# Layer-1 weight streams: the up weights of the feed-forward stage move from SP plus a VectorE cast to a casting load on POOL, the query weights of attention the other way

## What is computed

```
xn = layernorm(x)                                   # 2048 tokens x 1024
qkv = xn @ W_qkv + b_qkv                            # 16 heads of 64
s = softmax(q k^T / 8 + causal mask) v @ W_out + b_out
gate = xn @ (w_gate/127).T ; up = xn @ (w_up/127).T  # w_*: int32, hidden 3072
g = silu( (silu(gate) * up) @ (w_down/127).T )
x = x + s * g
```

## Time and profile before

| | |
|---|---|
| timed runs, median of 3 | 5059.19 us (5056.44, 5059.19, 5265.64) |
| the profiled execution | 4858.27 us, span of its slowest core 4856.6 us |
| spans of the eight cores | 4834.3 to 4856.6 us, mean granted clock 0.902 to 0.918 |
| TensorE busy | 3579.9 us, 74% |
| VectorE / ScalarE / POOL busy | 1320.2 / 1328.9 / 258.5 us |
| B1, gate and up steps of the first half | 3356 to 3560 us |
| C1, heads | 4147 to 4811 us |

### The profile page before, as it was taken

The page is one execution under the profiler, slowest core; times in us unless marked ns, Lnnn a source line. Parts: engine busy times, 40 slices in busy tenths (PEclk is TensorE's granted clock), DMA queues, the critical chain, the costliest instruction groups (busy, mean ns, idle before and its releaser), DMA issues.

```text
span 4856.6 us, 44207 instructions; the slowest of 8 cores (4834.3 to 4856.6 us)
## 1 busy us (share of the span) xinstructions
PE 3579.9 (74%) x14422; PEld 1437.2 (30%) x14712; DVE 1320.2 (27%) x2124; ACT 1328.9 (27%) x1573; POOL 258.5 (5%) x474
## 2 busy tenths in 40 slices
PE   2246666799999999986777777734798876667776
PEld 0012222344444444432222222211343332122222
DVE  3333320033023113203222222234212112454433
ACT  1100000011011011103666666511111100356663
POOL 1000000000000000000000000010000000000000
PEclk9868888899999999998999999856999999899998
DMA  2256778744434434440011121144343321122212
GB/s 74 65 147 192 199 208 188 188 147 146 140 131 147 139 139 140 146 124 11 11 31 37 35 42 37 37 112 107 87 96 72 87 53 28 18 52 53 49 36 65
DMA packets 139087, 463.50 MB, mean 95 GB/s; under 512 B 15568, under 2 KB 15728, under 8 KB 122480
## 3 DMA queue, kind: packets, MB, share of 16 engines
q0 software_dynamic: 66720, 205.83, 20.7%
q1 hardware_dynamic: 72144, 254.84, 15.5%
HBM read 490.23 MB, written 73.40 MB: 116 GB/s over the span
## 4 chain that ended last, share of the span: by engine, by line
PE 55%; DMA 15%; DVE 14%; ACT 9%; issue 5%; DVEq 1%; another core or an unknown queue 1%; SPq 0%; ACTq 0%; POOL 0%; POOLq 0%
PE pst L747 8%; ACT a16t L1539 8%; PE pst L761 8%; PE pst L863 4%; PE pb L863 4%; DMA a32t<-l_u 4%; PE pst L952 4%; PE pst L963 3%; PE pb L1016 3%; PE pb L1479 3%; PE pst L1505 2%; PE pst L1510 2%; DMA a16t<-s_g 2%; PE pb L1484 2%; PE pst L1393 2%
## 5 line engine op out<-in xcount | busy, mean ns | idle before, releaser
L1539 ACT ACTIVATE a16t<-pst 128x1024 bf16<-128x1024 f32 x832 | 852.1, 1024 | 452.5 <-PE pst L1510 379.1
L747 PE MATMUL pst<-xn_sb,a16t 128*128 128x512 bf16 x2256 | 585.4, 403 | 200.5 <-DVE a16t L695 165.3
L761 PE MATMUL pst<-xn_sb,a16t 128*128 128x512 bf16 x2259 | 552.6, 386 | 2.8 <-issue 0.7
L782 DVE TENSOR_TENSOR a32t<-a32t,pst 128x512 f32<-128x512 f32 x256 | 176.2, 688 | 1120.9 <-PE pst L761 1107.6
L774 ACT ACTIVATE a32t<-pst 128x512 f32<-128x512 f32 x288 | 172.0, 597 | 1106.0 <-PE pst L747 1090.6
L1479 PE MATMUL pb<-a16t 128*65 128x512 bf16 x832 | 332.9, 400 | 178.4 <-DVE a16t L1556 89.7
L1505 PE MATMUL pst<-a16t 128*128 128x512 bf16 x799 | 325.3, 407 | 159.9 <-DVE a16t L1438 103.4
L747 PEld LDWEIGHTS pst<-xn_sb,a16t 128*128 128x128 bf16 x2304 | 226.6, 102 | 509.8 <-issue 286.3
L1510 PE MATMUL pst<-a16t 128*128 128x512 bf16 x819 | 334.7, 409 | 6.6 <-DVE a16t L1452 4.1
L1484 PE MATMUL pb<-a16t 128*65 128x512 bf16 x832 | 330.9, 398 | 0.0
L761 PEld LDWEIGHTS pst<-xn_sb,a16t 128*128 128x128 bf16 x2304 | 229.9, 100 | 288.5 <-issue 29.5
(11 more groups left out here) (156 smaller groups left out, 2734.5 us busy)
## 6 DMA issues: line engine op xcount, KB each, us to landing
a16t<-s_g POOLq DMA_DIRECT2D x108, 512.0 KB, 4.9
a16t<-s_u SPq DMA_DIRECT2D x108, 512.0 KB, 3.7
a32t<-l_u SPq DMA_DIRECT2D x32, 1024.0 KB, 10.5
a16t<-s_d SPq DMA_DIRECT2D x27, 1024.0 KB, 5.4
a16t<-s_d POOLq DMA_DIRECT2D x27, 1024.0 KB, 5.8
a32t<-l_u SPq DMA_DIRECT2D x48, 512.0 KB, 4.9
s_g<-a16t SPq DMA_DIRECT2D x36, 512.0 KB, 7.9
s_u<-a16t SPq DMA_DIRECT2D x36, 512.0 KB, 8.5
```

Of the source, the lines that this page charges most:

```text
L747: li = t.matmul(pb[gp_][:, :], a16t[:, o_gb[wp] + hc * 256 + ici * 128: o_gb[wp] + hc * 256 + ici * 128 + 128], xn_sb[:, hc * T + tc * TC: ...
L761: li = t.matmul(pb[up_][:, :], a16t[:, o_ub[wp] + hc * 256 + ici * 128: o_ub[wp] + hc * 256 + ici * 128 + 128], xn_sb[:, hc * T + tc * TC: ...
L1539: return s.activation(a16t[:, o_pt[kp4]:o_pt[kp4] + 2 * TC], pst[kp][:, 0:1024], AF.Exp, scale=0.125)
```

## The change

In B1 the up tile is loaded by POOL straight to bf16, directly behind the gate tile and on the same semaphore, waiting like it for the h of step ic-2. The two staging buffers and the 48 casts are gone, and SP issues no load in B1.

In C1 the query weights are loaded by SP as f32 into the one scratch area `o_rt`. The load waits for the previous pair's cast (and at qi = 0 for the end of B1). A cast on VectorE then writes the bf16 tile; it waits for the load and for what the POOL load waited for. The operations are added where the POOL load was added: on SP behind the store of the previous pair's group, on VectorE behind the previous pair's fuse and ahead of L1447. The projection waits for the cast. Layer 0 keeps its load. `sWu` is an existing pair of semaphores.

```diff
-            o_st1 = [a32.alloc(1024) for _ in range(2)]
...
-                    def f_ldur(q, usrc=usrc, wp=wp):
+                    def f_ldu(q, usrc=usrc, wp=wp):
                         if q is None:
                             return 1
                         return q.dma_start(
-                            out=a32t[:, o_st1[wp]:o_st1[wp] + 1024].bitcast(I32),
-                            in_=usrc)
+                            out=a16t[:, o_ub[wp]:o_ub[wp] + 1024], in_=usrc)
...
-                    opldur = P.add("Q", f_ldur,
-                                   deps=[prev.get(("st1", wp))] + fen,
-                                   sem=sWu[wp], name=f"B1ldur{sc}.{ic}")
-
-                    def f_ucast(v, wp=wp):
-                        with nc.allow_low_precision(reason="i32 weight -> bf16"):
-                            return v.tensor_copy(
-                                a16t[:, o_ub[wp]:o_ub[wp] + 1024],
-                                a32t[:, o_st1[wp]:o_st1[wp] + 1024].bitcast(I32))
-                    opldu = P.add("V", f_ucast, deps=[opldur, bp],
-                                  name=f"B1ucast{sc}.{ic}")
-                    prev[("st1", wp)] = opldu
+                    opldu = P.add("G", f_ldu, deps=[bp] + fen, sem=sW[wp],
+                                  name=f"B1ldu{sc}.{ic}")
...
                     dlq = [pv.get(("qbuf", qi - 2))]
                     if qc == 0 and p < 2:
                         dlq.append(pv.get(("kbuf", nkv - 2 + p)))
-                    opldq = P.add("G", f_ldwq, deps=dlq, sem=sQW[p % 2],
-                                  name=f"C{L}ldq{qc}.{p}")
+                    if L == 0:
...
+                    else:
+                        def f_ldwqr(q, qsrc=qsrc):
+                            if q is None:
+                                return 1
+                            return q.dma_start(
+                                out=a32t[:, o_rt:o_rt + 1024], in_=qsrc)
+                        dqr = [pv.get(("qstg",))]
+                        if qi == 0:
+                            dqr = dqr + fence
+                        opldqr = P.add("Q", f_ldwqr, deps=dqr, sem=sWu[p % 2],
+                                       name=f"C1ldqr{qc}.{p}")
+
+                        def f_qwc(v, wp=wp):
+                            with nc.allow_low_precision(reason="wq f32 -> bf16"):
+                                return v.tensor_copy(
+                                    a16t[:, o_wq[wp]:o_wq[wp] + 1024],
+                                    a32t[:, o_rt:o_rt + 1024])
+                        opldq = P.add("V", f_qwc, deps=[opldqr] + dlq,
+                                      name=f"C1qwc{qc}.{p}")
+                        pv[("qstg",)] = opldq
```

More of the change, by code:

```diff
@@ L1378, in phase_C @@
                     qsrc = wq_src[p]
[L1380 to L1384, removed]
                     dlq = [pv.get(("qbuf", qi - 2))]
@@ L1387, in phase_C, with f_ldwq @@
                         dlq.append(pv.get(("kbuf", nkv - 2 + p)))
-                    opldq = P.add("G", f_ldwq, deps=dlq, sem=sQW[p % 2],
-                                  name=f"C{L}ldq{qc}.{p}")
+                    if L == 0:
+                        def f_ldwq(q, qsrc=qsrc, wp=wp):
+                            if q is None:
+                                return 1
+                            return q.dma_start(
+                                out=a16t[:, o_wq[wp]:o_wq[wp] + 1024], in_=qsrc)
+                        opldq = P.add("G", f_ldwq, deps=dlq, sem=sQW[p % 2],
+                                      name=f"C{L}ldq{qc}.{p}")
+                    else:
+                        def f_ldwqr(q, qsrc=qsrc):
+                            if q is None:
+                                return 1
+                            return q.dma_start(
+                                out=a32t[:, o_rt:o_rt + 1024], in_=qsrc)
[12 more added lines that the diff above has]
+                        pv[("qstg",)] = opldq
                     def f_qmm(t, wp=wp, qc=qc):
```

## The result

The changed kernel is slower: the ratio to the kernel before is 1.031 (95% interval 1.029 to 1.032). Each kernel was timed ten times: the medians are 5061.5 us (lowest 4999.6) and 4960.0 us (lowest 4846.3). Both medians contain executions in which one die of the chip ran at a lower clock, in shares that differ from kernel to kernel, so the ratio is taken from the undisturbed ones, which lie at 4846 to 4864 us before and at 5000 to 5012 us after: about 149 us more.

What follows compares the result with a forecast made beforehand. TensorE, busy 74% of the span, was taken as the bound, through its stops. B1 -80, C1 transfer +162, chunk 0 +5 and clock +46 gave +133 us, added to the 5059.2 us median: 5192 us, range 5120 to 5265.

Steps and rivals of the forecast that it cites:

- the last of the sum: Whole kernel: adds the same 133 us to the 5059.2 us median of three timed runs, giving 5192 us.
- B1, -80 us: Gate and up steps of B1: the wait for the cast goes, 1.74 us won in each of 46 steps.
- The term L: B1: time from POOL's first load issue to the landing of the second load, estimated at 5.7 us.
- the formula's two steps: B1: with two alternating buffers, two steps take 6.91 + 1.51 + L + 0.15 us, one step 4.29 + L/2.
- The bound from the only back-to-back pair, 6.6: B1: L = 6.6 from one pair of transfers on POOL's queue, a 7.59 us step and 59 us won.
- C1, the transfer laid open, 162 us: C1, query chunks 1 to 3: load behind the store, landing 4.2 us; 7 x 7.43 + 16 x 6.85 us.
- C1, the clock, 46 us: C1: TensorE's clock falls after the hole of about 8 us, 2.0 us in each of 23 pairs.
- The prediction's upper end (2.6): C1: clock cost up to 2.6 us a pair if the first scores still run at the low level.
- Chunk 0, 5 us: C1, query chunk 0: the cast alone is new, 0.44 us nine times and about 1 us once.
- The rival of the hidden load: C1: query load hidden, only the cast behind the fuse costs, 56 us; kernel 19 us faster, 5040 us; chance 0.05.
- The rival of two slow casting loads: B1: two casting loads on one queue, L = 7.9, only 29 us won; +184, 5243 us; chance 0.15.
- That the clock stays up: C1: clock stays up, load quick (3.7 us), B1 at its bound: +65, 5124 us, up to +95; chance 0.23.

Runs made afterwards that it cites:

- e7_nowo: Changed kernel without six of the eight loads of output projection weights in query chunk 1; ratio 1.032 (1.029 to 1.035), chunk 1 4.8 us shorter.
- the filler: Changed kernel plus 36 extra matmuls, results unused, on TensorE ahead of each of 23 query projections; ratio 1.021 (1.012 to 1.030).
- e2_c1only: Kernel before with only the C1 part of the change; no interval from timed runs, median span 5062.8 us, 220 us above the kernel before.
- e1_b1only: Kernel before with only the B1 part of the change, two buffers; ratio 0.980 (0.972 to 0.988), timed again 0.984.
- e3_prefetch: Changed kernel with SP issuing the query load one pair ahead, before the store, cast left in place; ratio 1.003 (0.998 to 1.009).
- e8_prewarm: Changed kernel with the query load a pair ahead, plus 14 extra matmuls on TensorE ahead of each of 23 query projections; ratio 0.998 (0.995 to 1.001).

## Why the prediction was right and wrong

**The forecast time, 5192 us, and its range, 5120 to 5265, missed the measured 5061.5.** The step that failed is the last of the sum: "the waits and transfers priced here are not tied to what makes those runs longer, so I add the same 133 us: 5192 us". The increase was near (133 us forecast, 147 to 149 measured), the base of 5059 us to which I added it was not. It was the median of three runs, 5056 to 5266 us, all far above the 4858 us of the profiled execution; of the seven later runs of the same kernel five lie between 4846 and 4864 us, and the median of all ten is 4960.0. With that base the same sum gives 5093 us and the same range 5021 to 5166, which holds 5061.5. On the profiled execution, from whose rows every term of the sum came, it gives 4991 us, beside the 5000 to 5012 us given above. As a ratio the forecast was 1.027 of the profiled execution, the measurement 1.031.

**B1, -80 us: right** (-78; -83 and -80 in the runs with B1 alone). The term L, from the first issue to the second landing, was put at 5.7 us; it is 0.51 + 5.1 = 5.6 (3435.15 to 3435.66 and the landing). The two alternating steps of the timeline, 7.17 us on average, are the formula's two steps. The bound from the only back-to-back pair, 6.6, was too high. Three buffers show the formula's other side: with a step more to land, the 6.91 us of TensorE are all that is left.

By the figures of the Trainium skill ("DMA: Bandwidth & Descriptors", "Anatomy of one DMA") an estimate for the pair was 4.4 us; the measured 5.6 us decides, and by that estimate the two-buffer version would have had no wait to lose and three buffers nothing to win, while they won 12.6 us.

**C1, the transfer laid open, 162 us: right.** With the median landings measured, 5.1 us in chunk 1 and 4.1 in chunks 2 and 3 where I took 4.2 for all, the same formula gives 7 x 8.33 + 16 x 6.75 = 166 us. The two landings miss 4.2 on opposite sides, which is why the sum is so close. The excess in chunk 1 comes mostly from the POOL load issued 1.7 us earlier (e7_nowo), which the prediction did not look for.

**C1, the clock, 46 us: right in kind, a little small.** By difference it is 221 - 166 = 55 us, by the filler 51, 2.2 to 2.4 us a pair. The projection alone takes 1.7 us longer (3.57 us in place of 1.89, median of the 23 pairs on all cores); the rest is put down to the low stretches behind the bias adds, which no run isolates. The prediction's upper end (2.6) had the low level last into the first scores; in the pair shown the clock rose in between and fell again.

**Chunk 0, 5 us: not shown.** It is 4.2 us longer, but only 0.7 us in e2_c1only, which has the same C1, and 1.9 us in e1_b1only, which has the old one. The agreement may be chance.

**The rival of the hidden load, 5040 us or 19 us faster, would have been wrong by its own edit.** Its terms were right (56 us without the clock), but I let the clock's price fall away with the long wait. The gap of 2.2 to 3.2 us that the cast alone leaves costs 47 us of clock: e3_prefetch is not faster than the kernel before.

**The rival of two slow casting loads** is excluded: L is 5.6, not 7.9. **That the clock stays up** is excluded by the 0.77 to 0.83 granted in chunks 1 to 3.

Two small things stay open, for which nothing was tried: what the change costs in chunk 0, where the versions with the changed C1 take 114 to 119 us and those with the old one 113 to 115, and what the remaining 0.3 us of landing in chunk 1 of e7_nowo is.

## What to carry to other kernels

On an engine or a queue that works in order, the price of an operation is its place. A cast behind the last multiply of a step cost 1.8 us a step; a load behind a store that waits for the end of a pair laid open a transfer that had been free; and the same 32 loads and 32 casts one pair earlier made the four query chunks 6 us longer in place of 225. For each moved load ask what stands ahead of it in its new queue and what that waits for.

Add to each new gap of TensorE the clock it costs, here 2 us for a gap of 2 to 3 us and 2.2 to 2.4 us for one of 7 to 9. And add a sum to the execution from whose rows its terms come: here the median of three runs stood 4% above it, and that alone put the forecast outside.

## What the runs showed of the hardware

- A TensorE gap of 2.2 to 3.2 us in every pair of 23 to 31 us, on top of the short gaps that were there, took the granted clock from 0.97 to about 0.85 (e3_prefetch), and 14 matmuls put into the gap brought it back to 0.99 and 0.97 in chunks 1 and 2 and to 0.94 in chunk 3 (e8_prewarm). I had expected the fall only for the 8 us gap.
- A 512 KB load on SP's queue without a cast landed in 3.7 us in chunk 0, where nothing is beside it, in 4.1 us behind a 256 KB store, and in 5.1 us when POOL had issued a load of output projection weights 1.7 us before.
- Two casting loads back to back on POOL's queue, 512 KB read each, land 4.4 and 5.1 us after their issues, the same as on two queues (4.5 for the gate tile on POOL, 4.9 for the up tile on SP). The Trainium skill ("SBUF — State Buffer", "SBUF: two separate sides") says that a fast VectorE cast holds up POOL's descriptors; the gate tile's landing went from 4.5 us with the cast beside its issue and the up load on SP to 4.4 us without the cast and with a second load behind it on POOL. No price shows, but no run here changes the cast alone.
